# Softplus attention in a two-layer block on one core: one softplus table pass in place of exponential, logarithm and maximum

## What is computed

```
# attention: 16 heads of 16
scores = einsum('bhqd,bhkd->bhqk', q, k) * hs ** (-0.5)
p = softplus(scores)
p = p * p
p = p * tril(ones)
attn = p / (sum(p, axis=-1, keepdims=True) + 1e-09)
out = einsum('bhqk,bhkd->bhqd', attn, v)

# experts: 8 of them, the best two for each token
gates = softmax(x @ gate_w.T + gate_b, axis=-1)
top_gates, top_idx = top_k(gates, 2)
expert_out = einsum('bsh,eoh->bseo', x, expert_w) + expert_b
y = (expert_out at top_idx * top_gates[..., None]).sum(axis=2)
```

## Time and profile before

| what | us |
|---|---|
| median of three runs | 1797.46 (1796.91 to 1798.94) |
| span of the profiled execution | 1794.8 |
| PE, DVE, ACT, POOL busy | 1683.5, 1295.7, 1092.9, 858.2 |
| attention stage | 274.4 to 815.2 |

### The profile page before, as it was taken

The page is one execution under the profiler, slowest core; times in us unless marked ns, Lnnn a source line. Parts: engine busy times, 40 slices in busy tenths (PEclk is TensorE's granted clock), DMA queues, the critical chain, the costliest instruction groups (busy, mean ns, idle before and its releaser), DMA issues. The chain is left out here.

```text
span 1794.8 us, 33269 instructions
## 1 busy us (share of the span) xinstructions
PE 1683.5 (94%) x11188; PEld 1158.1 (65%) x11188; DVE 1295.7 (72%) x2830; ACT 1092.9 (61%) x1612; POOL 858.2 (48%) x654
## 2 busy tenths in 40 slices
PE   8999897999999999998999899998899999889999
PEld 7888773333333333338788777777677777667777
DVE  5455885777777777775545788886787787778886
ACT  3332788999999999993333322214888887722120
POOL 0002108999999999995003322211265665411111
PEclk9999998999999999999999999999999999999999
DMA  5000275635535535400000100001232233200000
GB/s 164 1 0 12 91 214 90 76 48 73 68 47 73 67 47 79 62 1 1 13 1 30 29 7 0 0 0 39 83 96 95 104 112 103 95 1 24 23 23 24
DMA packets 57112, 95.09 MB, mean 53 GB/s; under 512 B 7904, under 2 KB 29632, under 8 KB 57024
## 3 DMA queue, kind: packets, MB, share of 16 engines
q1 hardware_dynamic: 56064, 93.35, 24.0%
q10 hardware_dynamic: 960, 0.59, 0.1%
HBM read 76.88 MB, written 17.04 MB: 52 GB/s over the span
## 5 line engine op out<-in xcount | busy, mean ns | idle before, releaser
L1508 POOL TENSOR_TENSOR att_weights<-att_weights 128x1024 f32<-128x1024 f32 (+1 forms) x288 | 508.9, 1799 | 9.0 <-DVE att_weights L1445 5.6
L1445 DVE SCALAR_TENSOR_TENSOR att_weights<-att_weights,ps 128x512 f32<-128x512 f32 x544 | 348.2, 684 | 145.1 <-ACT att_weights L1414 138.6
L932 DVE SCALAR_TENSOR_TENSOR X<-ps,moe_gsel,X 128x256 f32 (+1 forms) x512 | 246.6, 484 | 63.1 <-PE ps L48 44.8
L1369 PE MATMUL ps<-att_weights,att_v_ones 64*32 64x64 f32 (+5 forms) x2048 | 289.0, 399 | 1.9 <-POOL att_weights L1508 1.8
L1414 ACT ACTIVATE att_weights<-att_weights 128x1024 f32<-128x1024 f32 (+1 forms) x288 | 286.5, 1007 | 1.0
L1408 ACT ACTIVATE att_weights<-ps 128x1024 f32<-128x1024 f32 (+1 forms) x288 | 278.4, 972 | 8.6 <-PE ps L1349 7.0
L48 PE MATMUL ps<-w_experts_hi,moe_xh 128*128 128x512 f32 x512 | 205.3, 401 | 0.4 <-DVE X L932 0.4
L48 PE MATMUL ps<-w_experts_hi,moe_xl 128*128 128x512 f32 x512 | 203.2, 397 | 0.0
L48 PE MATMUL ps<-w_experts_lo,moe_xh 128*128 128x512 f32 x512 | 201.6, 394 | 0.0
L1369 PEld LDWEIGHTS ps<-att_weights,att_v_ones 128*32 128x32 f32 (+1 forms) x2048 | 82.4, 108 | 104.6 <-issue 80.2
L424 ACT ACTIVATE ffn_gates<-ps,ffn_gate_bias 128x512 f32<-128x512 f32 x72 | 49.5, 688 | 147.5 <-PE ps L48 143.2
(11 more groups left out here) (282 smaller groups left out, 3796.3 us busy)
## 6 DMA issues: line engine op xcount, KB each, us to landing
ssm_lb<-decays SPq DMA_DIRECT2D x32, 512.0 KB, 4.7
ssm_rise<-decays SPq DMA_DIRECT2D x28, 512.0 KB, 3.9
qk_parts<-qkv_part SPq DMA_DIRECT2D x32, 384.0 KB, 2.7
q_stack<-qk_parts SPq DMA_DIRECT2D x64, 128.0 KB, 4.9
k_stack<-qk_parts SPq DMA_DIRECT2D x64, 128.0 KB, 8.4
att_q_stack<-qk_parts SPq DMA_DIRECT2D x64, 128.0 KB, 4.7
att_k_stack<-qk_parts SPq DMA_DIRECT2D x64, 128.0 KB, 8.5
out<-X SPq DMA_DIRECT2D x7, 512.0 KB, 2.9
```

The lines of the kernel that those rows point to most:

```text
L932: dve.scalar_tensor_tensor(out=x, in0=ring[:, e // 2, (e % 2) * C:(e % 2 + 1) * C], scalar=gsel[:, s, j, e:e + 1], in1=x, op0=ALU.mult, op ...
L1369: ins = pe.matmul(O(qb)[h * 2 * HD:(h + 1) * 2 * HD, q0:q0 + w], values, Wt[rows, u % WU, t, c:c + w], start=kj == 0 and part == FULL, sto ...
L1445: dve.scalar_tensor_tensor(out=wt[:, t], in0=wt[:, t], scalar=LIMIT, in1=scores(u)[:, t], op0=ALU.min, op1=ALU.max).then_inc(max_done, 2 // n)
L1508: pool.tensor_tensor(wt, wt, wt, ALU.mult).then_inc(sq_pool, 1)
```

## The change

In attention, ACT applies one Softplus from its own table set and the maximum with its limit of 60 goes. The score slot is free, and the squares can start, when Softplus is done (`plus_done`). In each body POOL squares the units u with u mod 5 equal to 1 or 3 (14 of 36, all wide), DVE the others (18 wide, 4 narrow), at the place on its queue where the maximum was. In the experts, the two largest gates are struck out of a padded copy, and the comparison with the struck value makes the mask; `iota` and its load go. Every `Fori` becomes a Python `range`, so that all steps are written out with constants.

```diff
+SOFTPLUS_SET = "softplus"
...
-            with pe.Fori(1, BODIES - 1) as i:
+            for i in range(1, BODIES - 1):
                 body(i)
...
+    on_pool = lambda u: u % 5 in (1, 3)
+    pool_squares = [sum(on_pool(x) for x in range(u)) for u in range(NU + 1)]
+    dve_squares = [u - pool_squares[u] for u in range(NU + 1)]
...
-                half = -1
                 upper = segments[0][-1] == UPPER
+                pe.wait_ge(plus_done, i * NU + u + 1)
                 if upper:
                     low = slice(0, HALF)
-                    pe.wait_ge(max_done, 2 * (i * NU + u) + 1)
-                    pe.sem_inc(scores_free, 1)
...
-                    if t != half and not upper:
-                        half = t
-                        pe.wait_ge(max_done, 2 * (i * NU + u) + t + 1)
...
-                pe.wait_ge(sq_pool, i * NU + u + 1)
+                if on_pool(u):
+                    pe.wait_ge(sq_pool, i * pool_squares[NU] + pool_squares[u + 1])
+                else:
+                    pe.wait_ge(sq_dve, i * dve_squares[NU] + dve_squares[u + 1])
...
-            act.preload_act_table_set(LN_EXP_SET)
+            act.preload_act_table_set(SOFTPLUS_SET)
...
-                act.activation(Wt[:, u % WU, 0:n], scores(u)[:, 0:n], ACT.Exp).then_inc(exp_done, 1)
...
-                act.activation(wt, wt, ACT.Ln, bias=1.0).then_inc(ln_done, 1)
...
+                act.activation(Wt[:, u % WU, 0:n], scores(u)[:, 0:n], ACT.Softplus).then_inc(plus_done, 1)
...
-                for t in range(n):
-                    dve.scalar_tensor_tensor(out=wt[:, t], in0=wt[:, t], scalar=LIMIT, in1=scores(u)[:, t],
-                                             op0=ALU.min, op1=ALU.max).then_inc(max_done, 2 // n)
+            def square(i, u):
+
+                dve.wait_ge(plus_done, SU + i * NU + u + 1)
+                wt = Wt[:, u % WU, 0:BANKS[u % PU]]
+                dve.tensor_tensor(wt, wt, wt, ALU.mult).then_inc(sq_dve, 1)
...
-                    softplus(i, u)
+                    if not on_pool(u):
+                        square(i, u)
...
-                    pool.wait_ge(max_done, 2 * (SU + i * NU + u + 1))
-                    wt = Wt[:, u % WU, 0:BANKS[u % PU]]
-                    pool.tensor_tensor(wt, wt, wt, ALU.mult).then_inc(sq_pool, 1)
+                    if on_pool(u):
+                        pool.wait_ge(plus_done, SU + i * NU + u + 1)
+                        wt = Wt[:, u % WU, 0:BANKS[u % PU]]
+                        pool.tensor_tensor(wt, wt, wt, ALU.mult).then_inc(sq_pool, 1)
```

The new choice, in `choose`, with two memsets at the start of the phase:

```diff
-                dve.drain()
+                ins.then_inc(best_done, 1)
+                dve.wait_ge(best_done, n + 1)
+                dve.tensor_copy(wanted[:, :, 0:2], best[:, :, 0:2]).then_inc(wanted_done, 1)
+                dve.wait_ge(wanted_done, n + 1)
                 for j in range(GT):
-                    ins = dve.max_index(place[:, j], best[:, j], prob[:, j])
-                ins.then_inc(place_done, 1)
...
-                dve.tensor_copy(placef[:, :, :], place[:, :, 0:2]).then_inc(placef_done, 1)
...
-                for r in range(2):
-                    ins = dve.tensor_tensor(pick[:, r], iota[:, :].unsqueeze(1).broadcast_to([P, GT, E]),
-                                            placef[:, :, r:r + 1].broadcast_to([P, GT, E]), ALU.is_equal)
...
-                dve.tensor_tensor(pick[:, 0], pick[:, 0], pick[:, 1], ALU.add).then_inc(both_done, 1)
...
-                dve.tensor_tensor(gsel[:, s], half[:, :, :], pick[:, 0], ALU.mult).then_inc(gsel_done, 1)
+                    ins = dve.match_replace(struck[:, j], wanted[:, j], prob[:, j], STRUCK)
+                ins.then_inc(struck_done, 1)
+                dve.wait_ge(struck_done, n + 1)
+                dve.scalar_tensor_tensor(out=gsel[:, s], in0=struck[:, :, 0:E], scalar=STRUCK, in1=half[:, :, :],
+                                         op0=ALU.is_equal, op1=ALU.mult).then_inc(gsel_done, 1)
...
+            dve.memset(prob[:, :, E:2 * E], PAD)
+            dve.memset(wanted[:, :, :], PAD).then_inc(pads_set, 1)
```

More of the change, by code:

```diff
@@ L10 @@
 BF16 = mybir.dt.bfloat16
-U32 = mybir.dt.uint32
 ALU = mybir.AluOpType
@@ L397, in _ @@
             step(0, first=True)
-            with pe.Fori(1, B - 1) as i:
+            for i in range(1, B - 1):
                 step(i)
@@ L433, in _ @@
             step(0, first=True)
-            with act.Fori(1, B - 1) as i:
+            for i in range(1, B - 1):
                 step(i)
@@ L512, in _ @@
             step(0, first=True)
-            with dve.Fori(1, B - 1) as i:
+            for i in range(1, B - 1):
                 step(i)
@@ L527, in _ @@
             norm.pool_rstd(pool, 1, 1)
-            with pool.Fori(1, GROUPS // 2) as i:
+            for i in range(1, GROUPS // 2):
                 for s in range(2):
@@ L696, in moe_phase @@
     (eh, el), (gh, gl) = W
-    gate_b, bias3, iota = small
+    gate_b, bias3 = small
     CHUNKS = E * C // BANK
+    PAD, STRUCK = -1.0, -2.0
     with Phase(nc) as ctx:
@@ L805, in _ @@
             group(0, 0)
-            with pe.Fori(0, GROUPS // 2 - 1) as i:
+            for i in range(0, GROUPS // 2 - 1):
                 group(i * 2 + 1, 1)
@@ L868, in _ @@
             apply(1, 1)
-            with act.Fori(0, GROUPS // 2 - 1) as i:
+            for i in range(0, GROUPS // 2 - 1):
                 group(i * 2, 0)
@@ L893, in choose @@
                 dve.wait_ge(rec_done, n + 1)
[L894 removed]
+                dve.tensor_tensor(prob[:, :, 0:E], ex[:, :, :], total[:, :].unsqueeze(2).broadcast_to([P, GT, E]),
                                   ALU.mult).then_inc(prob_done, 1)
                 dve.wait_ge(prob_done, n + 1)
[L897 removed]
+                dve.tensor_scalar(half[:, :, :], prob[:, :, 0:E], 0.5, None, ALU.mult)
@@ L972, in _ @@
             dve.wait_ge(g3_zero, 1)
+            dve.wait_ge(pads_set, 1)
             choose(0, 0)
-            with dve.Fori(0, GROUPS // 2 - 1) as i:
+            for i in range(0, GROUPS // 2 - 1):
                 group(i * 2, 0)
@@ L1016, in _ @@
             split.split(pool)
-            with pool.Fori(0, GROUPS // 2 - 2) as i:
+            for i in range(0, GROUPS // 2 - 2):
                 group(i * 2, 0)
@@ L1087, in steps @@
             step(1, 0, 1, 3)
-            with eng.Fori(1, B - 2) as i:
+            for i in range(1, B - 2):
                 step(i * 2, i, 0, 3)
@@ L1213, in _ @@
             norm.pool_shift(pool, 1, 1)
-            with pool.Fori(0, GROUPS // 2 - 1) as i:
+            for i in range(0, GROUPS // 2 - 1):
                 for h in range(HALVES):
@@ L1235, in _ @@
                 load_stacks(sp, stacks, loaded, parts_dram, 0, 0, STACKED[n * share:(n + 1) * share])
-            with sp.Fori(2, B) as i:
+            for i in range(2, B):
                 for h, u in places:
@@ L1407, in exp @@
                 n = BANKS[u % PU]
-                act.activation(Wt[:, u % WU, 0:n], scores(u)[:, 0:n], ACT.Exp).then_inc(exp_done, 1)
-            def ln(i, u):
-                i, u = i + u // NU, u % NU
-                act.wait_ge(exp_done, i * NU + u + 1)
-                wt = Wt[:, u % WU, 0:BANKS[u % PU]]
-                act.activation(wt, wt, ACT.Ln, bias=1.0).then_inc(ln_done, 1)
[L1416 to L1426, removed]
+                act.activation(Wt[:, u % WU, 0:n], scores(u)[:, 0:n], ACT.Softplus).then_inc(plus_done, 1)
             act.sem_inc(o_turned, 2)
@@ L1430, in _ @@
             act.sem_inc(pv_done, NS)
[L1431 to L1435, removed]
+            act.sem_inc(plus_done, SU)
+            for i in range(BODIES):
+                for u in range(NU):
+                    softplus(i, u)
         @block.vector
         def _(dve):
[L1439 to L1443, removed]
-                for t in range(n):
-                    dve.scalar_tensor_tensor(out=wt[:, t], in0=wt[:, t], scalar=LIMIT, in1=scores(u)[:, t],
-                                             op0=ALU.min, op1=ALU.max).then_inc(max_done, 2 // n)
+            def square(i, u):
+                dve.wait_ge(plus_done, SU + i * NU + u + 1)
+                wt = Wt[:, u % WU, 0:BANKS[u % PU]]
+                dve.tensor_tensor(wt, wt, wt, ALU.mult).then_inc(sq_dve, 1)
             def copy_output(n, i, k):
@@ L1479, in body @@
                     outputs_left(BLOCK_UNITS, NU, OUT_LAG, i, divide_output)
-            dve.sem_inc(max_done, 2 * SU)
             body(0, first=True)
-            with dve.Fori(1, BODIES - 1) as i:
+            for i in range(1, BODIES - 1):
                 body(i)
@@ L1514, in _ @@
             copy_v(0, 0, 0)
-            with pool.Fori(0, BODIES - 1) as i:
+            for i in range(0, BODIES - 1):
                 body(i)
@@ L1521, in _ @@
             load_stacks(sp, stacks, loaded, parts_dram, 0, 1, STACKED)
-            with sp.Fori(1, BODIES) as i:
+            for i in range(1, BODIES):
                 for s in range(2):
@@ L1559, in _ @@
             copy_in(0, 1)
```

(16 more changed lines are left out.)

31 lines of the change are left out of this document (10 added, 21 removed).

## The result

The changed kernel takes **1731.22 us** (median of four runs, 1729.37 to 1732.38), the kernel before, beside it, 1798.20 (1796.91 to 1799.43): a ratio of 0.9629, 95% interval 0.9617 to 0.9642. The forecast was 1739 in a range of 1718 to 1767. The span of the profiled execution fell from 1794.8 to 1728.2, by 66.6 us, where the prediction's sum was 58.

The account below looks back on a forecast made before the run. The prediction took ACT to bound attention, with PE next after the change. Attention bodies -51, prologue -5 and written-out loops -2 made -58 us, giving 1739 us against a median of 1797.46, in a range of 1718 to 1767.

Parts of the forecast that it names:

- ACT sets the pace and POOL is close behind: Attention loop before the change: ACT's 32 wide Exp and Ln pairs, 66.4 us, were said to set the 66.66 us body.
- Softplus at one pass: ACT in attention: one wide Softplus was taken to cost 1.02 us, like Exp, with 2.07 us as upper bound.
- the rival's 71 us a body: ACT in attention: Softplus at 2.07 us keeps ACT the bound, 71 us a body, 1830 us in all; chance 0.05.
- PE's body of 57.9: PE in attention: scores 21.4, values 34.5 and turns 2.0 us make a 57.9 us body, against 66.66.
- Full exclusion: DVE and POOL squares in attention: each waits for the other to end; in series they are 51 us a body.
- The exposed wait: Attention block ends: PE's value unit waits for the division behind a DVE square, 2.4 us a body, making it 60.3.
- Choice at 0: Top-two choice in the experts: some 0.5 us less DVE time in each of 16 groups, worth 0 overall.
- A branch costs the stage nothing: Attention loops: straight-line first body 66.74 against the loop's 66.66 us; other phases' written-out loops give -2 together.
- within 2 us: Sign that the forecast is right: the stages before and behind attention stay within 2 us.
- the 1720 given: Rival in attention: no exclusion and no exposed wait, bodies of 57.9 us, another 19 us less, 1720; chance 0.17.
- Squares did not run late: Rival in attention: squares fall behind and PE waits at value units, 1767 to 1797 us; chance 0.13.
- stalls at fetches: Rival for the written-out loops: engines stall fetching code and eat the gain, around 1795 us; chance 0.03.

## Why the prediction was right, point by point

- **What bounds the kernel: half wrong.** "ACT sets the pace and POOL is close behind" is the wrong way round, by 65.47 against 64.09. The step that failed took 66.4 us from ACT's durations and called the overlap little. The 66.4 count the 32 wide pairs alone; with the four narrow ones, of 592 and 633 ns, the durations add up to 71.3, where ACT at its limit took 64.09: the overlap is some 7 us a body. The sum did not suffer, since the change takes work off both.
- **Softplus at one pass: right**, 1024 ns for the 1.02 taken. The page "ScalarE activation tables: per-element evaluation and per-set limits" of the Trainium skill (What a function is on this engine) has the table make no difference; the 1024 beside 1020 agree. Two passes as two instructions cost 39 us over the changed kernel and stay under the kernel before; the rival's 71 us a body, and its 1830, added up durations without their overlap. What one instruction of 2.07 us would have cost was not run.
- **PE's body of 57.9: right**, 58.18 where nothing waits for a division. Unit prices read from start to start, in stretches without a wait, added up to within 0.3 us.
- **Full exclusion: right**, for squares of one tile too. Squares stretch from 1222 to 1604 ns, and the one that comes second does nearly all its work behind the first. The page "SBUF — State Buffer" of the Trainium skill (Who interferes with whom) calls the ports that the two engines share an exclusive lock; the 1.08 us behind POOL's end, in 72 squares of 72, agrees.
- **The exposed wait: right in kind and place, a little dear.** Predicted 0.77 + 1.6 = 2.4 us a body; removing it gave 1.93. PE was there at 2.14 us, not 2.05, and the divisions ended at 2.56 and 3.53 where 2.82 and some 3.65 were taken; the value units started at 2.62 and 3.58, after 0.5 and 1.4 of waiting. The smaller wait and PE's larger body nearly cancel: 60.11 for 60.3.
- **Attention: -60.7 for -56.** The prologue gave 5.95 (5), seven bodies 46.8 (44.5), the last body with its tail 8.0 (6.4). Why the tail gave more was not tried.
- **Choice at 0: wrong**, 1.4 us. Its 0.5 us less DVE time was near the 0.6 of the second M phase, and the step "44.8/16 = 2.8 us a group covers them" held there; it failed at the first group of the first M phase, where the old choice ran beside POOL's products and took 1.8 us longer than the new one. **"A branch costs the stage nothing": wrong**, 0.4 us a body, because the first body stood for a body without a loop; with all loops written out it takes 67.2 us (287.09 to 354.31) and the ones behind it 66.25, and on POOL, where the 0.4 us lie, it was in the loop. **Outside attention: -5.9 for -2**: 1.4 from the choice, 0.6 from the loops of the last phase, 3.4 in the scan phase with its cause open, so that the sign "within 2 us" failed there; the last half microsecond, most of it in the first M phase, was not traced.
- **The rivals.** Without the exposed wait the time is 1714.75, near the 1720 given, but the exclusion is there; it was the order of the queue that could be had for nothing. Squares did not run late: 13.5 us of short waits for DVE's and 3.0 for POOL's in the stage. Written-out loops alone made the kernel no slower, so stalls at fetches ate no gain. The upper end of the range, 1767, was added up from the span of 1794.8 and not from the median; from the median it is 1770. Nothing hung on it.

## What to carry to other kernels

Two engines that are both nearly full have to be relieved together: here each half alone was worth 0.8 and 2.2 us of a body's 66, both 6.1. Read an engine's limit from the starts of its instructions when it never waits, not from the sum of their durations. When a change shifts the bound to another engine, look for the short dependent steps that this engine waits for, and put them ahead of the long, patient work on their queue: one line moved gave some 15 us more.

## What the runs showed of the hardware that was not expected

POOL's side of the contention is as large as DVE's. A value copy takes 609 ns where DVE does not square (L1473 in the run with all squares on POOL) and 1598 in the changed kernel; the half-sized one 395 and 1314. The square keeps its 1.89 us when it comes first, and a wide DVE square its 1.16 to 1.23. Whoever issues first pays nothing, so a one-unit shift of the assignment moved a microsecond from a square that PE waits for to one that nobody does. And consecutive ACT instructions overlap: 1.04 and 1.08 us long, they start 0.90 and 0.95 apart.
